# First half of the layer norm statistics finished in the stage ahead, at five stage boundaries

## What is computed

```python
def _layernorm(x, axis=-1, eps=1e-05):
    m = jnp.mean(x, axis=axis, keepdims=True)
    v = jnp.var(x, axis=axis, keepdims=True)
    return (x - m) / jnp.sqrt(v + eps)

    x = x + _L0_xattn_ref(_layernorm(x, axis=-1), ctx_1024, ...)
    x = x + _L0_ffn_ref(_layernorm(x, axis=-1), ...)        # low-rank experts
    x = x + _L1_xattn_ref(_layernorm(x, axis=-1), ctx_1024, ...)
    x = x + _L1_ffn_ref(_layernorm(x, axis=-1), ...)        # mixture of 16 experts
    x = x + _L2_xattn_ref(_layernorm(x, axis=-1), ctx_1024, ..., mask_Bx1xSxS2_ff0, ...)
    x = x + _L2_ffn_ref(_layernorm(x, axis=-1), ...)        # channel mix
    x = x + _L3_xattn_ref(_layernorm(x, axis=-1), ctx_1024, ..., mask_SxS2_bk1, ...)
    x = x + _L3_ffn_ref(_layernorm(x, axis=-1), ...)        # two layers of local attention and a gated MLP
```

## Time and profile before

| | us |
|---|---|
| median of 3 runs | 3204.5 |
| the runs | 3196.86, 3204.50, 3204.99 |
| the profiled execution | 3204.94 |
| its span, first to last instruction | 3203.2 |
| PE busy | 2953.5 (92%) |
| DVE busy | 2415.4 (75%) |
| ACT busy | 1617.7 (51%) |
| POOL busy | 1146.5 (36%) |
| mean granted PE clock, share of 2.4 GHz | 0.958 |

### The profile page before, as it was taken

One profiled execution on the slowest core, in us unless ns is written; L12 is line 12 of the kernel. 1 busy time (PEld: TensorE's weight loads), 2 busy tenths in 40 slices (PEclk: granted clock), 3 DMA queues, 4 the chain that ended last, 5 costly groups with the idle time before them and its releaser, 6 DMA issues. The chain is left out here.

```text
span 3203.2 us, 101205 instructions
## 1 busy us (share of the span) xinstructions
PE 2953.5 (92%) x37168; PEld 2076.8 (65%) x37200; DVE 2415.4 (75%) x5273; ACT 1617.7 (51%) x2596; POOL 1146.5 (36%) x1289
## 2 busy tenths in 40 slices
PE   6998779997999989998899969999988999999989
PEld 4776657775666657776667746666665566766655
DVE  6887768886777757776678868888876588888756
ACT  3665226663333335554356665666653356666523
POOL 4210322110000011110211208888872278888734
PEclk9999769998999989998999989999999999999999
DMA  3311001110000011210011110000001100000022
GB/s 94 92 40 24 7 11 30 31 30 15 0 0 0 0 24 41 42 40 21 7 32 46 43 33 10 8 10 10 6 4 33 26 8 10 10 9 7 4 81 76
DMA packets 190888, 81.28 MB, mean 25 GB/s; under 512 B 175953, under 2 KB 176528, under 8 KB 190240
## 3 DMA queue, kind: packets, MB, share of 16 engines
q1 hardware_dynamic: 187024, 69.14, 9.3%
q0 software_dynamic: 3728, 10.28, 0.9%
HBM read 37.55 MB, written 8.39 MB: 14 GB/s over the span
## 5 line engine op out<-in xcount | busy, mean ns | idle before, releaser
L596 POOL TENSOR_TENSOR x_norm<-x,mean_all 128x512 f32 (+1 forms) x80 | 83.1, 1039 | 1392.4 <-PE ps_pj L547 783.0
L889 ACT ACTIVATE probs_t<-ps_pt 128x1024 f32<-128x1024 f32 x256 | 262.0, 1023 | 333.9 <-PE ps_pt L1003 332.8
L763 DVE TENSOR_REDUCE row_max<-ps_s 128x16 f32<-128x1024 f32 x256 | 312.5, 1221 | 122.4 <-PE ps_s L992 121.9
L2133 POOL TENSOR_TENSOR kblk<-kblk 128x1024 f32<-128x1024 f32 x128 | 302.1, 2360 | 140.9 <-DVE kblk L2176 140.8
L769 DVE TENSOR_TENSOR probs<-ps_s,row_max 128x1024 f32<-128x1024 f32 x256 | 313.4, 1224 | 16.2
L1025 PEld LDWEIGHTS ps_o<-v,probs_t 128*64 128x64 f32 x8192 | 259.7, 138 | 51.7 <-issue 37.1
L1025 PE MATMUL ps_o<-v,probs_t 128*64 128x18 f32 x8192 | 285.1, 212 | 0.2
L1003 PE MATMUL ps_pt<-ident,probs 128*128 128x128 f32 x2048 | 281.3, 281 | 0.0
L884 ACT ACTIVATE probs<-probs 128x1024 f32<-128x1024 f32 x256 | 268.4, 1049 | 11.8 <-DVE probs L769 11.7
L2146 POOL TENSOR_TENSOR kblk<-kblk,small_d 128x1024 f32<-128x1024 f32 x128 | 243.5, 1902 | 19.0 <-POOL small_d L2143 17.7
L1003 PEld LDWEIGHTS ps_pt<-ident,probs 128*128 128x128 f32 x2048 | 226.8, 143 | 28.8 <-issue 22.6
(11 more groups left out here) (336 smaller groups left out, 6621.8 us busy)
## 6 DMA issues: line engine op xcount, KB each, us to landing
ci<-in_ctx_t SPq DMA_DIRECT2D x64, 256.0 KB, 3.0
kblk<-k_t SPq DMA_DIRECT2D x688, 16.0 KB
ci<-x SPq DMA_DIRECT2D x64, 128.0 KB
ci<-x SPq DMA_DIRECT2D x128, 63.0 KB
x<-in_x_in SPq DMA_DIRECT2D x4, 1024.0 KB, 8.7
mask<-in_mask_l SPq DMA_DIRECT2D x64, 64.0 KB, 2.5
out<-x SPq DMA_DIRECT2D x16, 256.0 KB, 2.0
out<-x POOLq DMA_DIRECT2D x16, 256.0 KB, 2.3
```

The lines of the kernel that those rows point to most:

```text
L763: dve.tensor_reduce(by_group(row_max[u % 2][:, :]), scores_4, AX, ALU.max)\
L889: act.activation(probs_t[:, :, :], ps_pt[:, :, :].rearrange("p a (r t) -> p (a r) t", t=P), ACT.Copy).then_inc(pt_ready.sem, 1)
L2133: pool.tensor_tensor(a, a, b_, ALU.add).then_inc(rotated.sem, 1)
```

## The change

In its last group a stage finishes the statistics of the first 32 tiles (`HALF_TILES`), which belong to groups 0 to 7: `half_variances` and `half_newton` on DVE, `half_roots` on ACT, on columns 0 to 31 of the same tensors and with semaphores of their own. That is in all four attention stages and in the low-rank stage. Five stages use it and finish only columns 32 to 63 at their start: low-rank experts, L1 attention, mixture, channel mix, `normalise_residual`. (L0, L2 and L3 attention still do all 64 at their start; the mixture and the channel mix do no half.) At the end of the L0 attention and of the low-rank stage POOL also normalises group 0 of the stage to come (`normalise_next`), so that this stage's POOL begins with group 1. In the mixture and the channel mix `norm_window(0)` moves ahead of the rest of the statistics.

```diff
+        def half_variances(dve):
+            dve.wait_ge(x_norm_ready.sem, x_norm_ready.at(GROUPS, 0))
+            dve.wait_ge(carried.sem, carried.at(GROUPS // 2, 0))
+            variances(dve, chain_half, slice(0, HALF_TILES))
+        def half_roots(act):
+            roots_of(act, chain_half, roots_half, slice(0, HALF_TILES))
+        def half_newton(dve):
+            newton_of(dve, chain_half, roots_half, slice(0, HALF_TILES))
+        def normalise_next(pool):
+            pool.wait_ge(chain_half.sem, chain_half.at(0, 11))
+            pool.wait_ge(xt_in_psum.sem, xt_in_psum.at(GROUPS, 0))
+            normalise_window(pool, 0, GROUPS)
...
 # cross_attention, POOL
-                        normalise_rows(pool, g)
+                        if not (done and isinstance(g, int) and g == 0):
+                            normalise_rows(pool, g)
...
-                    pool.wait_ge(chain_all.sem, chain_all.at(0, 11))
+                    if not done:
+                        pool.wait_ge(chain_all.sem, chain_all.at(0, 11))
                     for g in range(unrolled):
                         body(g)
...
+                    if done:
+                        pool.wait_ge(chain_all.sem, chain_all.at(0, 11))
                     with pool.Fori(unrolled, GROUPS) as g:
                         body(g)
+                    if norm_next:
+                        normalise_next(pool)
 # cross_attention, DVE
                             keep_stats(g, 1)
+                            if is_last(g):
+                                half_variances(dve)
                             divide(g, 3)
                             add_residual(g, 2)
                             keep_stats(g, 2)
+                            if is_last(g):
+                                half_newton(dve)
...
-                    all_variances(dve)
-                    all_newton(dve)
+                    all_variances(dve, done)
+                    all_newton(dve, done)
 # cross_attention, ACT
                             o_transposed(g, 2)
+                            if is_last(g):
+                                half_roots(act)
 # low_rank_experts, ACT
                             copy_gates(g)
+                        if is_last(g):
+                            half_roots(act)
 # low_rank_experts, POOL
                     pool.wait_ge(chain_all.sem, chain_all.at(0, 11))
-                    normalise_rows(pool, 0)
                     normalise_rows(pool, 1)
                     with pool.Fori(2, GROUPS) as g:
                         normalise_rows(pool, g, (norm_ready, logit_ready))
+                    normalise_next(pool)
 # low_rank_experts, DVE
+                        if is_last(g):
+                            half_variances(dve)
                         if has(g):
                             residual(g)
+                        if is_last(g):
+                            half_newton(dve)
...
 # mixture, ACT and DVE
-                    all_roots(act)
                     copy_x_transposed(act, 0, 0, None, 0)
+                    all_roots(act, HALF_TILES)
...
-                    all_variances(dve)
-                    all_newton(dve)
                     norm_window(dve, 0)
+                    all_variances(dve, HALF_TILES)
+                    all_newton(dve, HALF_TILES)
 # channel_mix, DVE
+                        if isinstance(g, int) and g == -1:
+                            all_newton(dve, HALF_TILES)
...
-        cross_attention("L0", 1.0 / np.sqrt(HD), ahead=1)
+        cross_attention("L0", 1.0 / np.sqrt(HD), ahead=1, norm_next=True)
...
-        cross_attention("L1", 1.0 / np.sqrt(HD), mask=masks["L1"])
+        cross_attention("L1", 1.0 / np.sqrt(HD), mask=masks["L1"], done=HALF_TILES)
```

More of the change, by code:

```diff
@@ L475, in all_roots, with variances @@
[L475 to L489, removed]
+        def variances(dve, chain, cols):
+            step = Steps(dve, chain, 0)
+            mean_, gap_, dev_ = mean_all[:, cols], gap_all[:, cols], dev_all[:, cols]
+            step(dve.tensor_tensor(mean_, stats_all[:, cols, 1], stats_all[:, cols, 4], ALU.add))
+            step(dve.tensor_tensor(gap_, stats_all[:, cols, 1], stats_all[:, cols, 4], ALU.subtract))
+            step(dve.tensor_tensor(dev_, stats_all[:, cols, 2], stats_all[:, cols, 5], ALU.add))
+            step(dve.tensor_scalar(mean_, mean_, 0.5, None, ALU.mult))
+            step(dve.tensor_tensor(gap_, gap_, gap_, ALU.mult))
+            step(dve.tensor_scalar(dev_, dev_, 1.0 / P, LN_EPS, ALU.mult, ALU.add))
+            step(dve.scalar_tensor_tensor(out=dev_, in0=gap_, scalar=0.25, in1=dev_, op0=ALU.mult, op1=ALU.add))
@@ new lines, in roots_of, with newton_of @@
+        def roots_of(act, chain, roots, cols):
+            act.wait_ge(chain.sem, chain.at(0, 7))
+            act.activation(log_all[:, cols], dev_all[:, cols], ACT.Ln).then_inc(roots.sem, 1)
+            act.wait_ge(roots.sem, roots.at(0, 1))
+            act.activation(root_all[:, cols], log_all[:, cols], ACT.Exp, scale=-0.5).then_inc(roots.sem, 1)
+        def newton_of(dve, chain, roots, cols):
+            step = Steps(dve, chain, 0, 7)
+            root_, work, dev_ = root_all[:, cols], work_all[:, cols], dev_all[:, cols]
+            dve.wait_ge(roots.sem, roots.at(0, 2))
+            step(dve.tensor_tensor(work, root_, root_, ALU.mult))
+            step(dve.tensor_tensor(work, work, dev_, ALU.mult))
+            step(dve.tensor_scalar(work, work, -0.5, 1.5, ALU.mult, ALU.add))
+            step(dve.tensor_tensor(rstd_all[:, cols], root_, work, ALU.mult))
@@ L493, in open_all, with open_half, is_last, normalise_window @@
             roots_all.opens(0, 2)
+        def open_half():
+            chain_half.opens(0, 11)
+            roots_half.opens(0, 2)
+        def is_last(g):
+            return isinstance(g, int) and g == GROUPS - 1
+        def normalise_window(pool, g, count):
+            spread = [P, GT, P]
+            pool.tensor_tensor(x_norm[:, :, :], x[:, bass.ds(g * GT, GT), :],
+                               mean_all[:, bass.ds(g * GT, GT)].unsqueeze(2).broadcast_to(spread),
+                               ALU.subtract).then_inc(x_norm_ready.sem, 1)
+            pool.wait_ge(x_norm_ready.sem, x_norm_ready.at(count, 1))
+            pool.tensor_tensor(x_norm[:, :, :], x_norm[:, :, :],
+                               rstd_all[:, bass.ds(g * GT, GT)].unsqueeze(2).broadcast_to(spread),
+                               ALU.mult).then_inc(x_norm_ready.sem, 1)
         def norm_tile(dve, g, u):
```

43 lines of the change are left out of this document (22 added, 21 removed).

## The result

| kernel | median, us | lowest to highest | runs | ratio to before, 95% interval | profiled span |
|---|---|---|---|---|---|
| before | 3199.61 | 3196.35 to 3204.99 | 22 | | 3203.2 |
| after | 3207.39 | 3201.72 to 3215.73 | 22 | 1.0023 [1.0016, 1.0030] | 3209.3 |

The change is no difference by the 0.3% bound, and yet a loss that the interval separates from nothing: 0.23%, 7.4 us. The forecast was a gain of 0.3 us, 3204.6. The time lies in the range, but the working behind it misses some 7.7 us. The ratios leave out two executions at a lower granted clock, one of before (4842.19 us at 0.551) and one of e12 (3443.39 us at 0.824).

What follows compares the result with a forecast made beforehand. It took the bare statistics chain, 3.54 us before the mixture's normalisation, as the main boundary cost, mostly covered elsewhere. Boundaries summed +1.67 + 1.46 - 3.33 + 0 - 0.14 = -0.34 us, from 3204.94 to 3204.6; range 3194 to 3211.5.

Steps and rivals of the forecast that it cites:

- The high end, 3211.5: Whole kernel: 3204.6 plus 1.7 for POOL's arrival and DVE delays plus 5.2 for the clock.
- the 5.2 us set aside for the clock: Low-rank stage: shifted start may change which groups run slow; four groups, 5.2 us, allowed to either side.
- the two rivals by the clock: Low-rank stage: two slow groups become fast, mixture's PE too, 3200.1 us, chance 0.12; three groups slower, 3208.5, chance 0.12.
- Step 1: L0 to prepare_low_rank: POOL ends at 310.13, next block opens 1.67 us later than before, nothing won in low-rank; +1.67.
- The bound: Ends of L0 and low-rank: POOL's arrival costs at most 0.72 us more each, +1.4; +1.7 with DVE delays.
- POOL does not hold the barrier: Rival at the ends of L0 and low-rank: POOL's work there delays no opening; -3.4, 3201.6 us, chance 0.10.
- Step 2: Low-rank to L1: POOL ends the stage 2.44 us later, L1's first transpose wins 0.98; +1.46.
- Step 3: L1 to mixture: 3.54 us won by normalising at once, 0.21 lost at L1's end; -3.33.
- it does not do what it says: Rival at the mixture's start: something hidden holds normalisation or router product, the 3.54 stay; 3208.1 us, chance 0.06.
- Steps 4 and 5: L2 to channel mix: covered, 0. L3 to normalise_residual: 0.13 lost, ACT's chain earlier; -0.14.
- The price of the small instructions: Half statistics on 32 columns: 0.03 us less per DVE instruction; seven take 1.65 us, four 0.84.
- the +1.5 by it: All five boundaries: halves priced as wholes, by the chained-instruction rule, make the sum +1.5, 3206.4 us.

Runs made afterwards that it cites:

- e12: Against before: half statistics in L1's last group alone, so only the mixture starts with them (repeat of e4); 3196.06 us, ratio 0.9985.
- e7: Changed kernel with the late loads that POOL issues moved from L0's first groups into a block of their own ahead of L0; 3238.67 us, one run.
- e8: Changed kernel with harmless POOL-issued transfers added: 4 in L1, 16 in L2, 51 in L3; 3210.0 us, one run.
- e2: Changed kernel without POOL's normalisation at L0's end, done in the low-rank stage again; 3201.44 us, ratio 1.0007.
- e5: Changed kernel without GpSimd's closing drain in L0's block and the short late-loads block behind it; 3203.43 us, ratio 1.0011.
- e11: e4's kernel with the half statistics of the last groups of L2 and L3 added; 3196.63 us, ratio to before 0.9991.
- e10: e4's kernel with half statistics in the low-rank stage's last group added, L1's POOL normalising group 0 itself; 3197.89 us, ratio to before 0.9991.
- e4: Against before: half statistics in L1's last group alone, so only the mixture starts with them; 3196.12 us, ratio 0.9992.
- e6: Changed kernel with half statistics at all five boundaries but POOL's early normalisation at neither stage end; 3201.89 us, ratio to before 1.0007.

## Why the prediction was right or wrong

**The time and the class were right by width and by luck, the account was not.** Forecast -0.3 us, measured +7.4 us by the ratio (interval 5.1 to 9.6). The high end, 3211.5, held it by the 5.2 us set aside for the clock in the low-rank stage, which is not where the time went: from the first residual to the last that stage took 109.5 us after and 109.1 before, with the same two groups of 8.0 us. So neither of the two rivals by the clock came true in the stage that they name; the clock cost something at L1's start and end. And the range was laid round 3204.9, where before's median is 3199.6: counted from its own base the high end is +6.6 us, less than the measured +7.4.

**Step 1, L0's end: the arrival was right, the price behind it was the failed term.** POOL was to end at 310.13 and ended at 310.15. That it fits to 0.02 is luck: the last quotient came at 306.05, where the sum has 305.47 + 0.22, and POOL's end followed in 4.10 us, not 4.44. But POOL ended 1.49 us behind DVE, and the sum has 310.13 - 308.46 - 0.22 = 1.45. The sum had the opening follow POOL's end as it had followed DVE's, 0.72 later, and it came 4.85 later. The bound said "If its arrival costs more than DVE's, I bound that by the longest gap here, 0.72 more at each of the two". That was a bound drawn from gaps that DVE ended, and it failed by a factor of six: what POOL has behind its last instruction was not in any row I read, because it was hidden and is not among the instructions that the views show. It is the closing drain: 4.17 us behind POOL's last instruction, and e7 and e8 tie it to the 50 transfers issued in the block, 0.08 us each; the other 0.68 of the gap are near the 0.72 that the same two block ends took before. The trace of before had the fact in its raw records (the same 4.17 us, at a place where nothing waited for POOL) and its cause in the code, the `late_loads` that POOL issues in L0's first ten groups; step 1 should have asked not only when POOL's instructions end but what POOL has to settle when its block closes. e2 and e5 together: 5.4 us for POOL's two instructions, of which 3.8 to 4.5 are this.

The rival "POOL does not hold the barrier" is out: it holds it, and with its drain longer than with its instructions. In the low-rank stage nothing was won, as said: the first key product waited for its context load and began 3.45 us after the start (325.09), 3.40 before.

**Step 2, low-rank to L1: both halves as forecast, the gain spent elsewhere.** From the end of the last residual to the opening 3.35 us (453.60 to 456.95) in place of 1.23 (447.34 to 448.57): +2.1 against +2.44. The barrier took 0.35, no 0.72 more. The first transpose waited for the bias copy and came 4.99 us after the start, forecast 5.08, before 6.06. That is 1.07 won at the first transpose, and L1 is yet 0.67 longer than before. Windows of L1's first 30 us, of before and of after (same columns):

```profile
448.57:458.57 10.00, 4.38 (x10) 0.50 0.24 53
458.57:468.57 10.00, 6.43 (x88) 0.67 0.13 28
468.57:478.57 10.00, 9.95 (x172) 0.93 0.01 2
```

```profile
456.95:466.95 10.00, 4.77 (x17) 0.50 0.24 54
466.95:476.95 10.00, 7.15 (x90) 0.50 0.13 28
476.95:486.95 10.00, 10.00 (x169) 0.87 0.01 2
```

The second ten us were all at 1.2 GHz, where before had a third of them at 2.4. The first `row_max` still starts 13.38 us after the stage's start against 14.46, with the lead whole; the second comes at 17.95 against 18.46, the third at 22.41 against 22.33, and the first tile's quotient at 24.81 against 24.73. The lead was gone before the loop was in its stride. That the clock took it is seen where the same instructions of L1 met another clock: in after 22.6 of the first 30 us were at 1.2 GHz, in e7 19.3, and e7's quotient comes at 24.22, half a us ahead of before; in e12 18.0, in e11 22.3, and the quotient at 24.73 and 25.43. e10, whose POOL normalises in L1 itself, had a lead of 0.4 only (first transpose at 5.64 against 6.06) and a clock like before's, and its quotient comes at 24.45. The prediction named this clock as a risk, but in the low-rank stage, and took a lead at a first transpose as a gain of the stage: that is this step's failed term, 0.98 won in the sum, nothing in the run. Why the clock rose later is not shown.

**Step 3, the mixture: right.** 3.16 us shorter against 3.54 won, router product 4.97 after the start against 4.90. L1's last group lost more than the 0.21 forecast: from the last quotient to the last residual 2.44 us (752.38 to 754.82), before 1.92 (743.85 to 745.77). TensorE's part of it, of before and of after:

```profile
744.58 0.30 PE L1012 MATMUL ps_pt<-ident,o 128*128 128x128 f32 x1 [0.82 <-DVE o L781]
...
745.25 0.49 PE L1033 MATMUL ps_o<-w_L_o,o_t 128*128 128x128 f32 x2 [0.37 <-ACT o_t L895]
```

```profile
753.11 0.45 PE L1072 MATMUL ps_pt<-ident,o 128*128 128x128 f32 x1 [0.94 <-DVE o L835]
...
753.92 0.80 PE L1093 MATMUL ps_o<-w_L_o,o_t 128*128 128x128 f32 x2 [0.37 <-ACT o_t L953]
```

In after the granted clock had fallen to 1.2 GHz at 752.6, before the last tile's turn, and the two steps took 0.46 us longer. In e12, with the same last group and the clock still at 2.4, the stretch is 1.99 us, 0.07 over before. e4 and e12 bear the step out by time: -2.6 and -4.8 us, forecast -3.33; the profiles of both have 1.7 to 1.9 us more from the channel mix's clock, so the stage's own rows size this step, and the medians only go with it. The rival "it does not do what it says" is out.

**Steps 4 and 5: right within 0.3.** L2 +0.02, channel mix +0.29; L3 +0.20; from the start of `normalise_residual` to TensorE's first instruction of the next stage 17.10 us against 17.49.

**The price of the small instructions was right.** 32 columns took 0.17 to 0.22 with POOL idle, seven of them from 456.95 to 458.54, 1.59 us, forecast 1.65; four from 459.17 to 460.03, 0.86, forecast 0.84. The halves so took 0.85 and 0.90 of what the wholes had taken: the rule that the prediction names from the Trainium skill, that the number of chained instructions counts, is right in kind, but the +1.5 by it lies far under the measured +7.4 too, whose cause is another.

**What adds up and what doesn't.** By the sum: -0.3 forecast, +4.1 for the drain (4.85 - 0.72), +1.1 for L1's lost lead, +0.3 for L1's last group make +5.2, at the low end of the measured interval. The table of stages has some more against the forecast: 0.4 each in the low-rank stage's loop and in the mixture, 0.3 in the channel mix. That is 6.3, as the two profiled executions differ (6.1), and the rest to 7.4 is within the interval. From the other side, e6 is 5.8 us over e12 and over e4 by the medians, 7.0 and 4.8 by the ratios. Of the 5.8, 1.5 are POOL and DVE side by side, 1.9 to 2.0 the channel mix's clock, 0.45 the clock in L1's last group, 0.6 by forecast, and 1.3 are open, with intervals of 3 us on each time.

## What to carry to other kernels

Before giving the last work of a stage to POOL, count the transfers that POOL issued in that block: its closing drain cost 0.08 us for each here, behind its last instruction and long after they had landed, and 50 of them made two instructions, 2.2 us long, cost over 5. In e5 it was hidden by leaving out the drain of that block and of the one behind it, so that it fell into one in which POOL was idle for long enough. And of several like edits, do the one whose wait is bare in the profile: the mixture's brought some 3 to 5 us alone, and of the four others none brought anything on top of it that these runs could tell from nothing. A lead at the start of a stage counts only if the clock rises in time for it.

## What the runs showed of the hardware

- GpSimd's closing drain grows in proportion to the transfers that the engine issued in the block. Behind the engine's last instruction it took 0.07 us with none, 0.42 with 4, 1.40 with 16, 4.17 with 50 and 4.26 with 51. Left out, it comes back at the end of the next block (4.99 us by the record where 0.05 stood).
- A DVE instruction of 0.2 us on 128x32 that starts beside a POOL instruction of 1.04 us on 128x512 ends with it: 0.94 us for one with two operands in SBUF, 0.91 for a `tensor_scalar` with one. Not all with one are held: L463, batch norm statistics of one tile, took its 0.29 at 308.37 beside POOL's L533, as did L849 at 308.04, which has one operand in PSUM.
- The same instructions at the start of a stage met TensorE's return to 2.4 GHz at different times: 99.03, 97.60 and 96.94 us for the channel mix in after, e7 and e11, and 0.6 to 0.7 us at L1's first quotient.
